# Embedding rows split into low and high 16 dims, VectorE adds the halves, four 16-row sums a block

## The reference

```
for i, (W, bias) in enumerate(params):              # W0: 200 x 1600, W1, W2: 200 x 4000
    x = einsum('bhd,bmd->bhmd', h, inputs).reshape(B, -1, D)
    y = relu(einsum('oi,bid->bod', W, x) + bias)
    h, direct = split(y, 2, axis=1)                 # the last layer: direct = y, all 200
    outs.append(direct)
z = concatenate(outs, axis=1).sum(-1)               # 512 x 400, summed over the 32 dims
h = concatenate([z, dense_ctx], axis=1)
y = relu(relu(h @ W_top1 + b_top1) @ W_top2 + b_top2) @ W_top3
```

## Time and profile before

| | us |
|---|---|
| median of 3 runs | 2891.62 (2888.71 to 2891.77) |
| the profiled execution | 2886.93 |
| its span | 2885.2 |
| PE busy | 2822.5 (98%) |
| DVE (VectorE) busy | 2600.9 (90%) |
| ACT (ScalarE) busy | 1502.3 (52%) |
| POOL (GpSimd) busy | 693.5 (24%) |

### The profile page before, as it was taken

One profiled execution on the slowest core, in us unless ns is written; L12 is line 12 of the kernel. 1 busy time (PEld: TensorE's weight loads), 2 busy tenths in 40 slices (PEclk: granted clock), 3 DMA queues, 4 the chain that ended last, 5 costly groups with the idle time before them and its releaser, 6 DMA issues.

```text
span 2885.2 us, 54840 instructions
## 1 busy us (share of the span) xinstructions
PE 2822.5 (98%) x19508; PEld 2805.9 (97%) x19508; DVE 2600.9 (90%) x1747; ACT 1502.3 (52%) x1880; POOL 693.5 (24%) x669
## 2 busy tenths in 40 slices
PE   3899999999999999999999999999999999999998
PEld 3899999999999999999999999999999999999996
DVE  5899999999999999999999999999999999999994
ACT  3555555555555555555555555555555555555553
POOL 2222222222222132222222122222222222222100
PEclk9999999999999999999999999999999999999999
DMA  6333433333333333333333334334333334334321
GB/s 185 87 86 76 101 82 79 96 83 80 96 83 82 93 82 85 93 80 88 89 78 92 89 76 95 85 76 98 86 74 98 86 74 101 84 76 99 89 63 24
DMA packets 280192, 250.13 MB, mean 87 GB/s; under 512 B 27711, under 2 KB 278687, under 8 KB 280066
## 3 DMA queue, kind: packets, MB, share of 16 engines
q1 hardware_dynamic: 211080, 196.64, 23.8%
q0 software_dynamic: 59744, 45.90, 11.0%
q10 hardware_dynamic: 9344, 7.27, 0.9%
HBM read 140.66 MB, written 4.20 MB: 50 GB/s over the span
## 4 chain that ended last, share of the span: by engine, by line
PE 85%; issue 11%; POOL 2%; DMA 2%; ACT 0%; SPq 0%; DVE 0%; POOLq 0%; DVEq 0%; ACTq 0%
PE acc L719 55%; PE acc L721 26%; PE z_ps L736 2%; PE hid_ps L732 1%; POOL gathered L412 1%; DMA x_pairs<-x_rows 1%; POOL wait_taker L420 1%; DMA acc_copy<-acc_copy 0%; PE acc L778 0%; PE hid_ps L801 0%; DVE product L661 0%; POOL acc_copy L421 0%; ACT heads L488 0%; DMA gathered<-in_table,rows_now 0%; SPq L302 0%
## 5 line engine op out<-in xcount | busy, mean ns | idle before, releaser
L719 PE MATMUL acc<-weights,heads 126*128 126x400 f32 (+1 forms) x9088 | 2704.0, 365 | 43.9 <-DVE tails L666 43.9
L721 PE MATMUL acc<-weights,tails 126*128 126x200 f32 (+1 forms) x9088 | 2322.8, 256 | 0.0
L488 ACT ACTIVATE heads<-product 126x1024 fp32r<-126x1024 f32 (+2 forms) x1152 | 1204.8, 1048 | 1149.7 <-PE acc L721 753.5
L719 PEld LDWEIGHTS acc<-weights,heads 126*128 126x128 f32 (+1 forms) x9088 | 1714.7, 189 | 45.6 <-issue 39.2
L721 PEld LDWEIGHTS acc<-weights,tails 126*128 126x128 f32 (+1 forms) x9088 | 1742.3, 192 | 0.0
L661 DVE TENSOR_TENSOR product<-hid_rep,x_rep 126x2048 f32<-126x2048 f32 x512 | 1172.5, 2290 | 205.8 <-PE acc L721 176.1
L666 DVE TENSOR_TENSOR tails<-product,heads 126x1024 fp32r<-126x1024 f32 (+2 forms) x1152 | 1338.9, 1204 | 6.6 <-ACT heads L488 6.5
L420 POOL TENSOR_TENSOR wait_taker<-wait_taker 1x1 f32<-1x1 f32 x192 | 115.8, 603 | 2046.9 <-ACT acc_copy L494 2045.3
L412 POOL DMA_INDIRECT gathered<-in_table,rows_now x150 | 316.7, 2111 | 45.7 <-issue 45.7
L499 ACT ACTIVATE y_relu<-acc_copy 128x400 f32<-128x400 f32 x192 | 102.4, 533 | 189.7 <-DMA acc_copy<-acc_copy 189.7
L421 POOL DMA_DIRECT2D acc_copy<-acc_copy x192 | 174.3, 908 | 1.3 <-issue 0.9
(11 more groups left out here) (21 smaller groups left out, 87.4 us busy)
## 6 DMA issues: line engine op xcount, KB each, us to landing
x_rep<-x_rows SPq DMA_DIRECT2D x512, 120.0 KB
hid_rep<-hid SPq DMA_DIRECT2D x512, 120.0 KB
x_pairs<-x_rows SPq DMA_DIRECT2D x192, 280.0 KB
acc_copy<-acc_copy POOLq DMA_DIRECT2D x192, 200.0 KB
hid_rep<-hid SPq DMA_DIRECT2D x512, 5.0 KB
x_pairs<-x_rows SPq DMA_DIRECT2D x64, 120.0 KB
raw_weights<-in_w ACTq DMA_DIRECT2D x12, 500.0 KB, 8.1
x_rep<-x_rows SPq DMA_DIRECT2D x128, 20.0 KB
```

The source lines that it names most:

```text
L488: act.activation(heads[0:rows, ring % HEADS_RING, 0:tiles, :], product[0:rows, ring % PRODUCT_RING, 0:tiles, :], ACT.Copy).then_inc(heads_ ...
L719: nc.tensor.matmul(acc[:, at.parity, c, 0:2 * LAYER], heads[0:rows, ring % HEADS_RING, k, cols], w, start=(q == 0 and k == 0), stop=False)
L721: last = nc.tensor.matmul(acc[:, at.parity, c, LAYER:2 * LAYER], tails[0:rows, ring % PRODUCT_RING, k, cols], w[:, 0:LAYER], start=False, ...
```

## The change

The two column groups of a block are no longer samples 0 to 3 and 4 to 7 but dims 0 to 15 and 16 to 31 of all 8 samples. Partition p of both groups then belongs to the same sample, so VectorE adds the two halves of `y_relu` (`fold`, giving `y_fold`, 128 x 200; for layers 0 and 1 only the direct 100 columns), and one matmul with `sum16` (128 x 8, ones for 16 rows each) takes the place of two with `sum32`: four a block. To lay the rows out so, the table is stored as two halves of 16 numbers a row, one under the other, and each gather fetches 128 half rows: five gathers a block where there were five for two blocks. GpSimd's loop is over blocks: an add, five gathers, the wait for them, two adds, two stores. The first four blocks are gathered ahead into four buffers (`FIRST`) and stored by SyncE, two of them before `load_pairs(0, 0)`.

In VectorE's order a fold stands: for the layer 2 slot of the iteration before, after tails 2 of layer 1; for layer 0, after tails 5 of layer 1; for layer 1, after tails 4 of layer 2.

```diff
+DIM_HALF = DIM // CG
+FLD_PART = 128 // (CG * BLOCK)
...
-            sp.wait_ge(first_gathered, GATHERS)
             store(0)
+            store(1)
             sp.wait_ge(first_stored[0], STORES)
             load_pairs(0, 0)
...
-                    sp.wait_ge(x_gathered, GATHERS)
-                    store(1)
+                    for b in range(2, FIRST):
+                        store(b)
...
+            with pool.Fori(FIRST, blocks) as b:
+                first = 1 + (b - FIRST) * 3
...
+                add(first)
                 for k in range(FLD_DMA):
-                    add(first + k)
                     gather(0, k, rows_now[:, k:k + 1], x_gathered)
+                pool.wait_ge(x_gathered, (b - (FIRST - 1)) * GATHERS)
+                add(first + 1)
+                add(first + 2)
+                for part in stored_parts(b, 0):
                     pool.dma_start(*part).then_inc(x_stored, 16)
...
+            def fold(layer, at, b):
+                first = HALF if layer < 2 else 0
+                dve.wait_ge(y_relued, at.slot + 1)
+                above_zero(dve, y_turned, at.slot)
+                dve.tensor_tensor(y_fold[:, first:LAYER], y_relu[:, 0, first:LAYER], y_relu[:, 1, first:LAYER],
+                                  ALU.add).then_inc(y_folded, 1)
...
+                        if first and layer == first[0] and q == 4 and before and before[0] > 0:
+                            between = before
+                        if second and layer == second[0] and q == 6:
+                            between = first
                         if previous[0]:
-                            make_previous_tails(at.group + q, at.ring + q)
+                            make_previous_tails(at.group + q, at.ring + q, between)
+                            if l0 and first and layer == first[0] and q == 6:
+                                fold(*l0)
...
+                pe.wait_ge(y_folded, at.slot + 1)
                 for n, first in enumerate((HALF,) if layer < 2 else (0, HALF)):
-                    for c in range(CG):
-                        at_col = n * BLOCK + c * (BLOCK // CG)
-                        last = nc.tensor.matmul(z_ps[0:HALF, at.parity, at_col:at_col + BLOCK // CG],
-                                                y_relu[:, c, first:first + HALF], sum32[:, :], start=True, stop=True)
+                    last = nc.tensor.matmul(z_ps[0:HALF, at.parity, n * BLOCK:(n + 1) * BLOCK],
+                                            y_fold[:, first:first + HALF], sum16[:, :], start=True, stop=True)
```

More of the change, by code:

```diff
@@ L70 @@
 EARLY_LOADS, AHEAD_LOADS = 3, 3
+FIRST = 4
 Q_PARTS = 4
@@ L76, in cin_kernel @@
 def cin_kernel(nc, ids, table, w0a, w0b, w1, w2, dense_t, wt1z, wt1d, wt2, wt3, bt1, bt2,
[L77 to L80, removed]
+               ident_in, sum16_in, ones_in, out):
+    blocks = ids.shape[1] - 1
+    batch = blocks * BLOCK
+    duos = blocks // 2
     assert blocks >= 6
@@ L426, in _ @@
             pool.wait_ge(rows_ready, 1)
-            for duo, gathers_done in ((0, first_gathered), (1, x_gathered)):
+            for b in range(FIRST):
                 for k in range(FLD_DMA):
-                    gather(duo, k, rows_all[:, duo, k:k + 1], gathers_done)
+                    gather(b, k, rows_all[:, b, k:k + 1], first_gathered[b])
             pool.wait_ge(first_stored[0], STORES)
             add(0)
[L433 to L438, removed]
+            for b in range(1, FIRST):
+                pool.wait_ge(first_stored[b], STORES)
@@ L447, in _ @@
-                pool.tensor_tensor(wait_taker[:, 2:3], wait_taker[:, 0:1], wait_taker[:, 0:1], ALU.add).then_inc(duos_stored, 1)
-                pool.wait_ge(duos_stored, duo - 1)
-            done = 1 + (duos - 2) * adds
+                pool.wait_ge(x_stored, (b - (FIRST - 1)) * STORES)
+                pool.tensor_tensor(wait_taker[:, 2:3], wait_taker[:, 0:1], wait_taker[:, 0:1], ALU.add).then_inc(blocks_stored, 1)
+                pool.wait_ge(blocks_stored, b)
+            done = 1 + (blocks - FIRST) * 3
@@ L671, in _, with make_previous_tails @@
             previous = [None]
-            def make_previous_tails(g, ring):
+            def fold(layer, at, b):
[4 more added lines that the diff above has]
+                                  ALU.add).then_inc(y_folded, 1)
+            def make_previous_tails(g, ring, between=None):
                 layer, q = previous[0]
-                for n in (2, 1):
-                    make_tails(layer, q + 2 - n, g - n, (ring - n) % RING)
+                make_tails(layer, q, g - 2, (ring - 2) % RING)
+                if between:
+                    fold(*between)
+                make_tails(layer, q + 1, g - 1, (ring - 1) % RING)
                 previous[0] = None
             def step(i, odd):
+                before, l0, l1, l2 = slots_of(i, odd)
+                first, second = (l1, l2) if l1 else (l2, None)
                 for layer in range(3):
@@ L693, in step @@
                             make_previous_tails(at.group + 2, at.ring + 2)
+                        if before and before[0] == 0 and layer == 0:
+                            fold(*before)
                         if odd is None:
@@ L699, in _ @@
             make_previous_tails(total_groups, total_groups)
+            fold(2, place(2, blocks - 1), blocks - 1)
         @block.tensor
@@ L828, in lay_out @@
     batch = arr("ids").shape[0]
-    ids = arr("ids").reshape(batch // DUO, DUO, FLD_DMA, FLD_PART).transpose(3, 1, 0, 2)
-    ids = ids.reshape(128, batch // DUO, FLD_DMA)
+    ids = arr("ids").reshape(batch // BLOCK, BLOCK, FLD_DMA, FLD_PART).transpose(3, 1, 0, 2)
+    ids = np.broadcast_to(ids[:, None], (FLD_PART, CG) + ids.shape[1:]).reshape(128, batch // BLOCK, FLD_DMA)
     packed = {"w0a": w0a, "w0b": w0b}
```

85 lines of the change are left out of this document (47 added, 38 removed).

## The result

| | us |
|---|---|
| before, median of 11 runs | 2891.77 (2888.71 to 2893.77) |
| the change, median of 11 runs | 2879.9 (2860.13 to 2887.76) |
| ratio, 95% interval | 0.9949 (0.9936 to 0.9963) |
| profiled execution of the change, its span | 2865.88, 2864.2 |

The change is faster by 0.5%, where 1.4% was forecast, and 2 us outside the range. Its executions spread over 27 us, those of before over 5. The profiled execution is near the fast end of the 27: it shows 21.0 us less span than before, of the 37.6 forecast.

A forecast was written before the change was run, and what follows sets the result against it. TensorE, busy 98% of the span, was taken as the bound. Terms -43.8 + 5.7 + 0.4 + 0.1 = -37.6 us gave 2849.3 from the profiled execution, 2854.0 from the median; 2852 was taken, range 2840 to 2878.

The forecast's parts named there:

- TensorE, -43.8: Eight of sixteen small matmul instructions a block go, 0.71 us a step; the first two steps' gain is lost: -43.8 us.
- VectorE's folds, 0.25 and 0.36 us, hidden: Three folds add 0.62 us a step on VectorE, 0.86 at most, covered by its idle time before products.
- Slack at the layer 2 turn: The layer 2 fold ends 0.27 us before TensorE's first sum weight load, less some 0.1 for the semaphore; the tightest spot.
- rival 1: TensorE waits for y_folded at the layer 2 turn: +6 to +25 us, 2858 to 2877; chance 0.16.
- GpSimd, "3.5 us are left: nothing": The batch of five gathers lands at 1441.2, ahead of layer 2's add, with 3.5 us left: no cost.
- rival 2: The gather batch makes layer 2's add late: +31 us, 2883, with every gather at the longest seen; chance 0.05.
- The fold as a wait in VectorE's queue: Each fold waits for its relu ahead of the next tails; at all three places no wait or hidden.
- Start, +5.7 and +0.4: First pair load waits for second gathers and store: +5.7 us (+4.5 to +7); first fold delays first sums: +0.4 (0 to 1).
- End, +0.1: At the end the last fold (0.36 and 0.1 for the semaphore) joins the path and 0.35 of matmuls goes: +0.1 us.
- Rival 3: Extra gathers hold up VectorE, a step of about 43.35 us instead of 42.84: +32, 2884 us; chance 0.04.

The follow-up runs named there:

- e10: e7 with each sum matmul issued twice, so 16 small TensorE instructions a block as before the change; median 2897.2 us.
- e2: e1 with a one-element memset, which reads nothing, in place of GpSimd's one-element add ahead of the accumulating DMA; median 2854.6 us.
- e7: The change with the layer 2 fold moved behind both tails and its turn on TensorE one group later; median 2854.3 us.
- e0: The changed kernel run again unaltered, for a second trace; median 2869.2 us.
- e5: The change with folds of the same size and place on unused data, no wait for the relu, sums of the low 16 dims only; median 2860.9 us.
- e3: The change without the folds, the sums taking only the low 16 dims; median 2851.4 us.
- e1: The change with GpSimd's loop written out, without the copy of the ids; median 3019.7 us.
- e13: The change with an idle 400-element ScalarE copy ahead of the copy that releases layer 0's add; median 2908.0 us.

## Why the prediction was wrong

By its own steps:

- **TensorE, -43.8:** right. 0.706 a step was measured against 0.71, in nearly every iteration, and e10 gives it back as 42.9. Eight columns cost nothing: the mean of L772 is 212 ns, that of the earlier trace rows 218.
- **VectorE's folds, 0.25 and 0.36 us, hidden:** right as durations (forms of 259 and 361 ns), and right that the idle time before products covers them: ordinary steps have TensorE busy throughout. That idle time fell by 1.5 us a step.
- **Slack at the layer 2 turn, rival 1:** right that it holds. TensorE waited for a fold 6.3 us in 4 waits over the whole span, the longest 3.6 and in the lockout of iteration 61, and not in ordinary iterations.
- **GpSimd, "3.5 us are left: nothing":** the step that failed. I compared the end of the batch of gathers with the add of layer 2, and there nothing went wrong: the gathers even became faster (mean 1.51 us, has a median of 2.11), and rival 2 did not occur (its sum had a slip: by its own terms it decides at a gather pitch of 3.41 us, not 3.55). I had also written "GpSimd is the one that waits", and took that wait for one VectorE operation, since the add of the earlier trace rows lasts 0.54 us and the gathers end at the next boundary. The sum had it at nothing, and no bound for it was put in the range. The runs show that with a short operation in VectorE's order the add can be passed over at three to five boundaries in a row, 5.3 to 6.5 us, mostly until VectorE stops at a fold. That costs 2.5 to 2.7 us an iteration in most cases at layer 0, 6.2 at layer 2, and 7.7 to 9.5 where a second one follows at layer 1. Lengthened iterations were 11.9 us in the one profiled execution and 30.9 in the other. By the medians it was 25 (2879.9 against 2854.6 in e2 and 2854.3 in e7), or 15 with the median of e0. That the wait has no bound of one operation stood in the trace of before, in the 7.64 us of iteration 2, which lies on its critical path; the prediction doesn't mention it.
- **The fold as a wait in VectorE's queue:** I checked each fold against its relu at the times of before. At layer 0 I said "over 1 us later"; that stands while the relu is on time, and the fold turns a late relu into a stop of VectorE of 3.69 us. In e5, without that wait, a lockout costs 1.8 us an iteration and not 2.6.
- **Start, +5.7 and +0.4:** first matmul at 34.39, where it was 30.02: +4.4, just under the lower bound, and the first sums waited 0.47 for the fold against 0.4. With three iterations of gain, iteration 5 starts 4.1 later where these terms gave 4.0.
- **End, +0.1:** wrong, +4.0 from the last layer 0 on, where -0.6 follows from my terms. The last iterations have no layer 0, the folds stand at the same places by group, and two come before their relu. TensorE then waits for the tails behind them, 1.8 and 1.3 us. An add of 2.94 us at 2791 isn't needed for it: e2, which has none, takes 139.9 us there too. e3 and e5, where no fold waits, take 136.7.
```profile
2774.61 0.37 DVE L693 TENSOR_TENSOR y_fold<-y_relu 128x200 f32<-128x200 f32 x1 [3.26 <-ACT y_relu L514]
...
2822.31 0.37 DVE L693 TENSOR_TENSOR y_fold<-y_relu 128x200 f32<-128x200 f32 x1 [2.77 <-ACT y_relu L514]
```
- **Rival 3, gathers or adds hold VectorE:** did not occur. Tails beside a gather last 1.22 us as without, products 2.29.

The Trainium skill (SBUF — State Buffer, "Who interferes with whom") says that a VectorE instruction with two SBUF inputs contends with GpSimd instructions that read SBUF, not with one that only writes. On this point e1 and e2 agree: the reading add was held up to 6.5 us, the memset at arrivals as bad never, 91 ns at the longest. The same section calls the shared ports an exclusive lock and says that issue order decides who blocks. It doesn't say who is let in next. I had read it as a wait for at most one VectorE operation, 2.3 us; the add was passed over at three boundaries in a row in iteration 54 and at four in iteration 61, so that reading is wrong here.

Open: why the boundaries refuse the add when it arrives in the last 0.13 us of a short operation or in the operation behind it, and when it arrives 0.5 to 0.9 us before the end of a product. The runs show when it happens, and that it is not certain (e1: 16 of 31), not how the ports are granted. The kind of iteration 61 is 6.2 of the 11.9 us of this execution and isn't explained. As a first lockout of a steady iteration it was seen once in the change and once in e13; all second ones at layer 1 and that of iteration 2 are of this kind too. The memset was tried only with the written-out loop; in the rolled one it was not.

## What to carry to other kernels

Before adding a short VectorE operation to a queue without gaps, list the GpSimd instructions with SBUF inputs on which a relu, a turn or a load depends, and find where they arrive. Look at the longest wait of such an instruction in the trace of before, not at a typical one: 7.64 us stood there beside 0.54. An instruction that only takes waits should read nothing (a memset of one element, as in e2), or the short operation should stand away from the arrival (in e7 the adds arrive 0.8 to 1.6 us before it). And a spread of runs that grows with a change (27 us, where before had 5 beside it and at most 13 in the later comparisons) is a finding: profile a second execution, since the first may be one of the good ones.

## What was not expected of the hardware

- A GpSimd addition of one element took 0.18 to 6.42 us in the change, up to 9.66 in e5; a memset of one element 88 to 91 ns in e2.
- Beside a busy VectorE it ends 0.04 to 0.05 us after the end of a VectorE operation, at the first such end or several later; VectorE itself isn't slowed by it (tails 1.22 us, products 2.29 with and without).
- Moving its arrival after the relu by 0.06, 0.2 and 0.37 us gave 2, 12 and 17 lockouts of 57 at layer 0, and 2863.5, 2892.8 and 2908.0 us.
- Five gathers in one batch took 1.51 us each in the mean, where each between two adds took 2.11.
